# Layer 3's product banks summed by GpSimd adds alone, beside moved spreads and merge

## The chip, the cores and the metric

The kernel runs on one core of one Trainium2 chip. The metric is the device time of one launch in microseconds, the median of several runs. The engines are named as in the profile: PE (TensorE), DVE (VectorE), ACT (ScalarE), POOL (GpSimd), and SP, which only issues transfers.

## The reference

A batch of 512 rows takes 48 embeddings of width 32 each, and passes them through three layers of a compressed interaction network. Each layer makes all products of its input's rows with the 48 original rows, multiplies them with a weight matrix and applies a relu. The sums over the width go through a small dense tower.

```python
def _cin_layer(xi, x0, W, b):
    Wr = W.reshape(Fi, F0, -1)
    out = jnp.einsum('nie,nje,ijo->noe', xi, x0, Wr) + b[None, :, None]
    return jax.nn.relu(out)
x0 = inputs                      # [512, 48, 32]
xs = [x0]
for W, b in ((W1, b1), (W2, b2), (W3, b3)):      # 128 outputs each
    xs.append(_cin_layer(xs[-1], x0, W, b))
return jnp.concatenate(xs, axis=1).sum(axis=-1)
```

## The kernel before

The work is cut into 128 tiles, one for each block of 128 batch rows (4) and each place in the width (32). A tile is a 128 x 48 slice `xx[:, t, :]` of scaled embeddings. Five engines each run the same software pipeline of steps `v` from -4 to 127. In step `v` layer 3 works on tile `v`, layer 2 on tile `v + 1`, layer 1 on tiles `v + 2` and `v + 3`. A step has 24 items, numbered `n`: items 0 to 11 are layer 2, items 12 to 23 are layer 3. In each item PE makes a bank `y` of 128 x 512 (four output groups, one for each of four original rows) in one of five PSUM banks (`RING = 5`), so PE can be at most five items ahead of whoever empties them.

In the code `layer` 0 is layer 2 and `layer` 1 is layer 3. Each bank has to be multiplied by four columns of `xx` and summed into 128 x 128. Two engines share this. `TAKES` says who takes which bank. For a bank of DVE's, four multiply-adds (`fma`) run from PSUM into one of two chains. For a bank of ACT's, `products` writes four scaled pieces into an SBUF buffer `work`, and POOL has to add the banks up. Layer 2 has six banks of ACT's (items 0, 2, 4, 6, 8, 10), layer 3 has five (items 13, 15, 17, 19, 21).

POOL's order in one step, written out by hand in `step` of the gpsimd block, is this:

- `sum_all(1, v - 1)`: finish the previous tile's layer 3 sum, once its DMA has landed (L359, L361, L368, L372)
- `add_by_dma(0, v + 1)`: an accumulating DMA that adds banks 2 and 3 of layer 2 to banks 0 and 1 (L332)
- `x0_scaled` in even steps (L400), and a gather of one embedding field for a later block in odd steps (L300), in steps 1 to 8 in the even ones too
- `sum_rest(0, v + 1)` (L343, L348, L351), and `x0_lo` in even steps (L405)
- `sum_all(0, v + 1)`: wait for the DMA, then L359, L361, L365, L372. The last one writes `psum` of layer 2
- `add_by_dma(1, v)` (L332), `squares_lo` (L394, one for each tile), another gather (L300), one `spread` of 8 tiles where a block has landed (L309, twelve in all), and `sum_rest(1, v)` (L348)

The 144 gathers of blocks 1 to 3 are given out one by one: two in each of steps -3 to 8, and then three in two steps, so that the last one is in step 88. A gather is an indirect DMA issued by POOL. A `spread` turns gathered rows around into tiles of `xx` and scales them; the first block's are made by DVE (L797).

DVE's `merge(layer, t, i)` adds the two chains and `psum`. The one of layer 2 stands at item 20. The one of layer 3's previous tile stands at item 9 (L859 and L864). ACT may write a product bank of the next tile only once `psum` of that layer is done (`s_sum`). PE may write bank `n` only once the bank five items before it is emptied (`bank_free`).

Of the kernel before, what the change touches and what calls it, by code (L numbers as in the profile page):

```python
# [30 lines left out]
F = len(ROWS)  # L31
E = 32
B = 512
P = 128
# [26 lines left out]
FOLDED = (P, 2 * P)  # L61
SUMS = [n + (w == P) for n, w in zip(NA, FOLDED)]
CHUNKS = (1, 0, 2, 3)
PIECES = 4
SPREAD, GROUP, EARLY = 8, 12, 8
# [15 lines left out]
def build(nc, ids, tables, ctx_in, select, pairs_of, w_pair, w_pair_t, w2, w3, b_cin, wt1, bt1, wt2, bt2, wt3, out):  # L81
# [3 lines left out]
    with ExitStack() as stack:  # L85
# [16 lines left out]
        emb = sb("emb", [P, NB, F, E])  # L102
# [19 lines left out]
        mx0, sc0 = sb("mx0", [P, 2, 2]), sb("sc0", [P, 2])  # L122
        mpsq, msq = sb("mpsq", [P, 2]), sb("msq", [P, 2])
# [19 lines left out]
        rest = [sb(f"rest{l}", [P, 2 * P]) for l in (2, 3)]  # L143
# [43 lines left out]
        s_xx = sem("xx_tiles")  # L187
# [7 lines left out]
        s_dma = [sem(f"products{l}_added") for l in (2, 3)]  # L195
        s_last = sem("last_sums")
# [100 lines left out]
        def _(pool):  # L297
            def gather(b, fields, landed=None):
                for f in fields:
                    pool.indirect_dma_start(  # L300
                        emb[:, b, f, :], None, tables[f],
                        bass.IndirectOffsetOnAxis(ap=ids_sb[:, b, f:f + 1], axis=0)).then_inc(landed or s_gather[b], 16)
# [17 lines left out]
            for f, landed in zip(range(0, F, GROUP), s_first):  # L320
                gather(0, range(f, f + GROUP), landed)

# [4 lines left out]
            def add_by_dma(layer, tile):  # L327


                p = prods[layer]  # L330
                written(layer, tile, 2 * ADDED - 1)
                pool.dma_start(p[:, 0:ADDED, :], p[:, ADDED:2 * ADDED, :], accum_op=ALU.add).then_inc(s_dma[layer], 16)  # L332

            def sum_rest(layer, tile):


                s, n = s_sum[layer], tile * SUMS[layer]
                a = prods[layer][:, 2 * ADDED, :]
                wait(pool, s, n)
                written(layer, tile, 2 * ADDED)  # L340
                for m in range(2 * ADDED + 1, NA[layer]):
                    written(layer, tile, m)
                    pool.tensor_tensor(part[layer][:], a, prods[layer][:, m, :], ALU.add).then_inc(s, 1)  # L343
                    a = part[layer][:]
                    n += 1
                    wait(pool, s, n)
                r = rest[layer]
                pool.tensor_tensor(r[:], a[:, 0:2 * P], a[:, 2 * P:4 * P], ALU.add).then_inc(s, 1)  # L348
                if FOLDED[layer] == P:
                    wait(pool, s, n + 1)  # L350
                    pool.tensor_tensor(r[:, 0:P], r[:, 0:P], r[:, P:2 * P], ALU.add).then_inc(s, 1)  # L351

            def sum_all(layer, tile):

                s, n = s_sum[layer], (tile + 1) * SUMS[layer] - 4
                p, a, w = prods[layer], part[layer], FOLDED[layer]
                wait(pool, s_dma[layer], (tile + 1) * 16)
# [5 lines left out]
                r = rest[layer][:, 0:w]  # L363
                if w == P:
                    pool.tensor_tensor(a[:, 0:P], a[:, 0:P], a[:, P:2 * P], ALU.add).then_inc(s, 1)  # L365
                    last = (a[:, 0:P], r)
                else:
                    pool.tensor_tensor(a[:, 0:2 * P], a[:, 0:2 * P], r, ALU.add).then_inc(s, 1)  # L368
                    last = (a[:, 0:P], a[:, P:2 * P])
                wait(pool, s, n + 3)  # L370
                wait(pool, s_m[layer], tile)
                pool.tensor_tensor(psum[layer][:], *last, ALU.add).then_inc(s, 1)  # L372

            def sum_last(layer, tile):


                p, a = prods[layer], part[layer]
                written(layer, tile, 1)
                wait(pool, s_sum[layer], tile * SUMS[layer])
                pool.tensor_tensor(a[:], p[:, 0, :], p[:, 1, :], ALU.add).then_inc(s_last, 1)  # L380
                for m in range(2, NA[layer]):
                    written(layer, tile, m)
                    wait(pool, s_last, m - 1)
                    pool.tensor_tensor(a[:], a[:], p[:, m, :], ALU.add).then_inc(s_last, 1)
                wait(pool, s_last, NA[layer] - 1)
                pool.tensor_tensor(a[:, 0:2 * P], a[:, 0:2 * P], a[:, 2 * P:4 * P], ALU.add).then_inc(s_last, 1)
                wait(pool, s_last, NA[layer])
                wait(pool, s_m[layer], tile)
                pool.tensor_tensor(psum[layer][:], a[:, 0:P], a[:, P:2 * P], ALU.add).then_inc(s_sum[layer], SUMS[layer])

# [18 lines left out]
            columns = [(b, e) for b in range(1, NB) for e in range(0, E, SPREAD)]  # L409
            given_out = {"rows": 0, "columns": 0}  # L410
# [8 lines left out]
            def next_spread(asked):  # L419


                i = given_out["columns"]
                if i < len(columns) and asked >= columns[i][0] * F:
                    spread(*columns[i], SPREAD)
                    given_out["columns"] += 1

            def step(v, parity):

                t0, t2, t3 = v + 3, v + 1, v
                asked = given_out["rows"]  # L430
                if active(t3 - 1):
                    sum_all(1, t3 - 1)
                if active(t2):
                    add_by_dma(0, t2)
                if parity == 0 and active(v + 4):
                    x0_scaled(v + 4)
                if v > 0 and (parity == 1 or v <= EARLY):
                    next_gather()
                if active(t2):
                    sum_rest(0, t2)  # L440
                if parity == 0 and active(v + 4):
                    x0_lo(v + 4)
                if active(t2):
                    sum_all(0, t2)
# [14 lines left out]
            sum_last(1, TILES - 1)  # L459
# [149 lines left out]
        def _(act):  # L609
# [73 lines left out]

            def save_turned(c):

                k = F + CTX if c == 0 else P
                act.wait_ge(s_tt, CHUNKS.index(c) + 1)
                nc.scalar.activation(hT[0:k, c, :], turned[c][0:k, :], ACT.Copy).then_inc(s_tts, 1)

            def step(v, parity):  # L690
# [5 lines left out]
                for n in range(2 * BANKS):  # L696
# [38 lines left out]
        def _(dve):  # L735
# [59 lines left out]
            def spread(g, e0, e1):  # L795
                fields = slice(g * GROUP, (g + 1) * GROUP)
                return nc.vector.tensor_scalar(xx[:, e0:e1, fields], emb[:, 0, fields, e0:e1].rearrange("p f e -> p e f"),  # L797
                                               wpow[:, 0:1], None, ALU.mult)

            for g in range(F // GROUP - 1):  # L800
                dve.wait_ge(s_first[g], 16 * GROUP)
                spread(g, 0, E)
            dve.wait_ge(s_first[F // GROUP - 1], 16 * GROUP)
            for e0, e1 in ((0, 4), (4, E)):
                spread(F // GROUP - 1, e0, e1).then_inc(s_xx, e1 - e0)
# [93 lines left out]
            def x0_over_e(b, i):  # L899
                fields = slice(i * F // PIECES, (i + 1) * F // PIECES)  # L900
                nc.vector.tensor_reduce(low[:, b, fields], emb[:, b, fields, :], axis=AX.X, op=ALU.add).then_inc(s_low, 1)

            def step(v, parity):
                t1, t2, t3 = v + 2, v + 1, v
                other = 1 - parity
                for n in range(2 * BANKS):
# [3 lines left out]
                    for k in range(Q):  # L910
# [20 lines left out]
                        if n == 11 and k == 0 and active(t3 - 1):  # L931
                            over_e(2, t3 - 1)
# [88 lines left out]
```

## Time and profile before

| What | us |
|---|---|
| median of 3 runs | 2412.47 |
| lowest and highest | 2411.84, 2414.49 |
| the profiled execution, its own time | 2416.4 |
| its span in the trace | 2414.6 |
| busy: PE, DVE, ACT, POOL | 2319.0, 2221.3, 2118.3, 1989.4 |

The own time lies 1.8 us over the span. Busy time of an engine counts the time in which an instruction runs. Register, branch and semaphore instructions don't count, and so a busy share below the whole can still leave no room.

### The profile page before, as it was taken

How to read it: one execution, taken by the hardware profiler on the slowest of the kernel's cores; microseconds unless marked ns; L12 is line 12 of the kernel's file. 1: busy time of each engine (PE TensorE's matmuls, PEld its weight loads, DVE VectorE, ACT ScalarE, POOL GpSimd, SP SyncE). 2: the span in 40 equal slices, each digit the busy share in tenths (PEclk: the TensorE clock that was granted, in tenths of full speed). 3: DMA queues.
4: the chain of work that ended last, by engine and by line, in shares of the span. 5: the costliest groups of instructions: out<-in, count | busy, mean ns of one | idle time of the engine just before them, and what ended most of it. 6: DMA issues, size and time to landing. Idle time of an engine off the chain costs nothing.

```text
span 2414.6 us, 67586 instructions
## 1 busy us (share of the span) xinstructions
PE 2319.0 (96%) x14174; PEld 1183.8 (49%) x14174; DVE 2221.3 (92%) x8840; ACT 2118.3 (88%) x7910; POOL 1989.4 (82%) x2262
## 2 busy tenths in 40 slices
PE   1699999999999999999999999999999999999999
PEld 0345555554455555555445555555445555555553
DVE  6499999999999999999999999999999999999995
ACT  4588999998899999899889999899899999999995
POOL 7588888888888888888888888888887777777774
PEclk6799999999999999999999999999999999999999
DMA  5133333333333333333333333333333333333331
GB/s 172 29 72 66 70 71 72 65 69 71 63 71 72 67 68 72 70 69 66 70 63 72 71 72 67 67 72 71 62 71 69 71 65 67 70 70 71 66 68 37
DMA packets 150185, 168.19 MB, mean 70 GB/s; under 512 B 111940, under 2 KB 115655, under 8 KB 150120
## 3 DMA queue, kind: packets, MB, share of 16 engines
q0 software_dynamic: 42864, 136.87, 30.6%
q1 hardware_dynamic: 107256, 30.73, 5.7%
q14 instruction: 57, 0.47, 0.1%
q8 instruction: 8, 0.13, 0.0%
HBM read 12.82 MB, written 0.00 MB: 5 GB/s over the span
## 4 chain that ended last, share of the span: by engine, by line
PE 75%; POOL 8%; issue 7%; ACT 6%; DMA 2%; SPq 1%; DVE 1%; ACTq 0%; DVEq 0%; POOLq 0%
PE y L519 64%; PE m L509 7%; ACT work L633 4%; PE m L491 2%; POOL part L359 2%; DMA work<-work 2%; POOL part L361 1%; POOL emb L300 1%; POOL rest L348 1%; DVE acc L850 1%; POOL work L332 1%; POOL part L343 1%; ACT work L663 1%; POOL psum L372 1%; POOL xx L309 0%
## 5 line engine op out<-in xcount | busy, mean ns | idle before, releaser
L519 PE MATMUL y<-whi,xT 128*128 128x512 f16 x6144 | 2001.2, 380 | 14.9 <-DVE acc L850 9.1
L633 ACT ACTIVATE work<-y,xc 128x128 f32<-128x128 f32 x5632 | 1614.7, 423 | 202.8 <-PE y L519 188.1
L850 DVE SCALAR_TENSOR_TENSOR acc<-y,xc,acc 128x128 f32<-128x128 f32 x5632 | 1628.6, 343 | 54.5 <-PE y L519 47.8
L519 PE MATMUL y<-wlo,xT 128*128 128x512 f16 x3072 | 1165.0, 379 | 0.0
L519 PEld LDWEIGHTS y<-whi,xT 128*128 128x128 f16 x6144 | 599.2, 98 | 658.1 <-issue 55.4
L519 PEld LDWEIGHTS y<-wlo,xT 128*128 128x128 f16 x3072 | 300.9, 98 | 229.1
L359 POOL TENSOR_TENSOR part<-work 128x512 f32<-128x512 f32 x255 | 324.2, 1271 | 68.4 <-DMA work<-work 45.3
L394 POOL TENSOR_TENSOR zl<-work,zh 128x1152 f16<-128x1152 f32 x128 | 344.4, 2691 | 8.1 <-ACT work L663 8.1
L332 POOL DMA_DIRECT2D work<-work x255 | 230.8, 905 | 104.7 <-ACT work L633 104.2
L300 POOL DMA_INDIRECT emb<-tbl,ids_sb x192 | 200.5, 1044 | 46.6 <-issue 45.2
L343 POOL TENSOR_TENSOR part<-work 128x512 f32<-128x512 f32 x128 | 163.6, 1278 | 88.1 <-ACT work L633 85.3
L661 ACT ACTIVATE zh<-m 128x512 f16<-128x512 f32 (+1 forms) x384 | 215.9, 562 | 3.0 <-PE m L491 3.0
L663 ACT ACTIVATE work<-m 128x512 f32<-128x512 f32 (+1 forms) x384 | 218.3, 568 | 0.0
L361 POOL TENSOR_TENSOR part<-part 128x256 f32<-128x256 f32 x255 | 185.6, 728 | 20.0
L491 PE MATMUL m<-x0T,sel 96*128 96x128 f16 x1280 | 136.0, 220 | 53.7 <-DMA x0T<-x0hl 43.7
L491 PEld LDWEIGHTS m<-x0T,sel 96*128 96x128 f16 x1280 | 103.2, 98 | 147.0 <-issue 50.7
L850 DVE SCALAR_TENSOR_TENSOR ends<-y,xc,acc 128x128 f32<-128x128 f32 x512 | 156.0, 351 | 0.0
L509 PE MATMUL m<-w1l,zh 128*128 128x128 f16 x1152 | 127.7, 220 | 0.0
L509 PEld LDWEIGHTS m<-w1l,zh 128*128 128x128 f16 x1152 | 92.0, 99 | 60.3 <-issue 0.8
L509 PEld LDWEIGHTS m<-w1h,zh 128*128 128x128 f16 x1152 | 87.0, 99 | 62.7 <-issue 2.2
L859 DVE TENSOR_TENSOR msum<-ends,psum 128x128 f32<-128x128 f32 x256 | 73.7, 288 | 45.7 <-POOL psum L372 40.6
L509 PE MATMUL m<-w1h,zh 128*128 128x128 f16 x1152 | 107.5, 221 | 1.3 <-ACT work L663 1.3
(108 smaller groups left out, 2141.8 us busy)
## 6 DMA issues: line engine op xcount, KB each, us to landing
work<-work POOLq DMA_DIRECT2D x255, 512.0 KB, 4.8
xT<-hi SPq DMA_TRANSPOSE x256, 2.2
xT<-lo SPq DMA_TRANSPOSE x256, 2.2
emb<-tbl,ids_sb POOLq DMA_INDIRECT x192, 2.5
xx<-w SPq DMA_DIRECT2D x4, 768.0 KB
work<-w SPq DMA_DIRECT2D x4, 768.0 KB
x0T<-x0hl SPq DMA_TRANSPOSE x128, 2.2
wt_sb<-W_top SPq DMA_DIRECT2D x1, 768.0 KB
```

The costliest lines, as they stand in the source:

```text
L300: pool.indirect_dma_start(emb[:, b, f, :], None, tables[f], bass.IndirectOffsetOnAxis(ap=ids_sb[:, b, f:f + 1], axis=0)).then_inc(landed o ...
L332: pool.dma_start(p[:, 0:ADDED, :], p[:, ADDED:2 * ADDED, :], accum_op=ALU.add).then_inc(s_dma[layer], 16)
L359: pool.tensor_tensor(a[:], p[:, 0, :], p[:, 1, :], ALU.add).then_inc(s, 1)
L361: pool.tensor_tensor(a[:, 0:2 * P], a[:, 0:2 * P], a[:, 2 * P:4 * P], ALU.add).then_inc(s, 1)
L394: pool.tensor_tensor(zl[:], zT[:, 0:KF, :], zh[:], ALU.subtract).then_inc(s_zl, 1)
L491: ins = nc.tensor.matmul(misc[PAIR_BANK[g]][:, (k % 4) * P:(k % 4 + 1) * P], sel[:, k * P:(k + 1) * P], x0T[0:2 * F, :], start=True, stop= ...
L509: ins = nc.tensor.matmul(misc[0][:, 0:P], z, w, start=i == 0, stop=i == L1_PASSES - 1)
L519: ins = nc.tensor.matmul(dst[:], xT[layer][:, parity, a, :], w[layer][:, cols], start=i == 0, stop=i == 2)
L633: nc.scalar.activation(prods[layer][:, a, k * P:(k + 1) * P], bank[:, k * P:(k + 1) * P], ACT.Copy, scale=xc[layer][:, parity, j:j + 1]).t ...
L661: nc.scalar.activation(zh[:, 4 * g:4 * g + n, :].rearrange("p t c -> p (t c)"), misc[PAIR_BANK[g]][:, 0:n * P], ACT.Square, scale=SQUARE)
L663: nc.scalar.activation(zT[:, 4 * g:4 * g + n, :].rearrange("p t c -> p (t c)"), misc[PAIR_BANK[g]][:, 0:n * P], ACT.Square, scale=SQUARE). ...
L850: ins = nc.vector.scalar_tensor_tensor(dst, y, col, mine, ALU.mult, ALU.add)
```

## The change

Three things change. The spreads leave POOL and DVE: `emb` is laid out so that all tiles of a field lie side by side, and ACT makes two tiles of `xx` in each odd step, behind its products of item 10, for the tiles `v + 5` and `v + 6`. POOL only raises a semaphore when a block has landed (three short memsets, and one for block 0). DVE makes just the first two tiles. The merge of layer 3 moves on DVE from item 9 to item 11, and `lo_part` by one place. And layer 3's accumulating DMA, `sum_rest` and `sum_all` go: `sum_banks` takes their place at the end of POOL's step. It adds the five banks one after the other into `part`, as ACT writes them, and folds the result twice. It is the order that `sum_last` had for the last tile alone.

```diff
-            def spread(b, e0, n):
-                t0 = b * E + e0
-                src = emb[:, b, :, e0:e0 + n].rearrange("p f e -> p e f")
-                pool.wait_ge(s_gather[b], 16 * F)
-                pool.tensor_scalar(xx[:, t0:t0 + n, :], src, wpow[:, 0:1], None, ALU.mult).then_inc(s_xx, n)
+            def block_landed():
+                pool.memset(flag[:], 0.0).then_inc(s_block, 1)
...
+            def sum_banks(tile):
+                s, n = s_sum[1], tile * SUMS[1]
+                p, a = prods[1], part[1]
+                wait(pool, s, n)
+                written(1, tile, 1)
+                pool.tensor_tensor(a[:], p[:, 0, :], p[:, 1, :], ALU.add).then_inc(s, 1)
+                for m in range(2, NA[1]):
+                    written(1, tile, m)
+                    wait(pool, s, n + m - 1)
+                    pool.tensor_tensor(a[:], a[:], p[:, m, :], ALU.add).then_inc(s, 1)
+                wait(pool, s, n + NA[1] - 1)
+                pool.tensor_tensor(a[:, 0:2 * P], a[:, 0:2 * P], a[:, 2 * P:4 * P], ALU.add).then_inc(s, 1)
+                wait(pool, s, n + NA[1])
+                wait(pool, s_m[1], tile)
+                pool.tensor_tensor(psum[1][:], a[:, 0:P], a[:, P:2 * P], ALU.add).then_inc(s, 1)
...
             def step(v, parity):
...
-                if active(t3 - 1):
-                    sum_all(1, t3 - 1)
                 if active(t2):
-                    add_by_dma(0, t2)
+                    add_by_dma(t2)
...
-                if active(t3) and t3 < TILES - 1:
-                    add_by_dma(1, t3)
                 if active(t0):
                     squares_lo(t0)
                 if v > -4:
                     next_gather()
                 if -4 < v <= 0:
                     next_gather()
-                next_spread(asked)
-                if active(t3) and t3 < TILES - 1:
-                    sum_rest(1, t3)
+                next_block(asked)
+                if active(t3):
+                    sum_banks(t3)
...
+            def spread(t):                       # on ACT
+                wait(act, s_block, (t >> 5) + 1)
+                wait(act, s_xx, t)
+                nc.scalar.activation(xx[:, bass.ds(t, 2), :], emb[:, :, bass.ds(t, 2)].rearrange("p f e -> p e f"),
+                                     ACT.Copy, scale=wpow[:, 0:1]).then_inc(s_xx, 2)
...
+                    if n == 10 and parity == 1 and active(v + 5):
+                        spread(v + 5)
...
-                        if n == 9 and k % 2 == 0 and active(t3 - 1):
-                            merge(1, t3 - 1, k // 2)
                         if n == 9 and active(t1):
-                            if k == 1:
+                            if k == 2:
                                 lo_part(0, t1)
...
-                        if n == 11 and k == 0 and active(t3 - 1):
-                            over_e(2, t3 - 1)
+                        if n == 11 and active(t3 - 1):
+                            if k in (0, 2):
+                                merge(1, t3 - 1, k // 2)
+                            if k == 3:
+                                over_e(2, t3 - 1)
```

The first place is on POOL, from the last instruction of layer 2's sum in one step to layer 2's DMA in the next, in a step of the middle of the program. Here is what stood there before. `part` and `rest` are POOL's partial sums, `psum` its result, `zl` the low part of the squares, and both DMAs on `work` are the accumulating ones.

```order
L372 TENSOR_TENSOR psum<-part,rest 128x128
L332 DMA work<-work 128x1024
L394 TENSOR_TENSOR zl<-work,zh 128x1152
L300 DMA emb<-tbl,ids_sb 128x32
L348 TENSOR_TENSOR rest<-work 128x256
L359 TENSOR_TENSOR part<-work 128x512
L361 TENSOR_TENSOR part<-part 128x256
L368 TENSOR_TENSOR part<-part,rest 128x256
L372 TENSOR_TENSOR psum<-part 128x128
L332 DMA work<-work 128x1024
```

And here is the same place now, with the changed kernel's line numbers.

```order
L364 TENSOR_TENSOR psum<-part,rest 128x128
L387 TENSOR_TENSOR zl<-work,zh 128x1152
L299 DMA emb<-tbl,ids_sb 128x32
L373 TENSOR_TENSOR part<-work 128x512
L377 TENSOR_TENSOR part<-part,work 128x512 x3
L379 TENSOR_TENSOR part<-part 128x256
L382 TENSOR_TENSOR psum<-part 128x128
L332 DMA work<-work 128x1024
```

One DMA, one add over 512 elements and three smaller adds have become four adds over 512 and two smaller ones.

The second place is on DVE, at items 9 and 11. `msum` and the second `ends<-ends,msum` are the two halves of layer 3's merge, `lo` is what layer 2's next input needs, and `acc` and `ends<-y` are the running multiply-adds. Before:

```order
L850 SCALAR_TENSOR_TENSOR acc<-y,xc,acc 128x128 x3
L859 TENSOR_TENSOR msum<-ends,psum 128x128
L850 SCALAR_TENSOR_TENSOR acc<-y,xc,acc 128x128
L890 SCALAR_TENSOR_TENSOR lo<-m,sc,hi 128x128
L850 SCALAR_TENSOR_TENSOR acc<-y,xc,acc 128x128
L864 TENSOR_TENSOR ends<-ends,msum 128x128
L850 SCALAR_TENSOR_TENSOR acc<-y,xc,acc 128x128
L897 SCALAR_TENSOR_TENSOR pooled<-m,pooled 128x128
L850 SCALAR_TENSOR_TENSOR acc<-y,xc,acc 128x128
L897 SCALAR_TENSOR_TENSOR pooled<-ends,pooled 128x128
```

Now:

```order
L844 SCALAR_TENSOR_TENSOR acc<-y,xc,acc 128x128 x5
L884 SCALAR_TENSOR_TENSOR lo<-m,sc,hi 128x128
L844 SCALAR_TENSOR_TENSOR acc<-y,xc,acc 128x128
L891 SCALAR_TENSOR_TENSOR pooled<-m,pooled 128x128
L844 SCALAR_TENSOR_TENSOR acc<-y,xc,acc 128x128
L853 TENSOR_TENSOR msum<-ends,psum 128x128
L844 SCALAR_TENSOR_TENSOR acc<-y,xc,acc 128x128
L844 SCALAR_TENSOR_TENSOR ends<-y,xc,acc 128x128
L858 TENSOR_TENSOR ends<-ends,msum 128x128
L844 SCALAR_TENSOR_TENSOR ends<-y,xc,acc 128x128
L891 SCALAR_TENSOR_TENSOR pooled<-ends,pooled 128x128
```

The merge stands four multiply-adds later than before, with nothing added.

## Rows read from the trace of the kernel before

**Rows 1.** The page: busy time, share and instructions of each engine.

```profile
PE 2319.0 (96%) x14174; PEld 1183.8 (49%) x14174; DVE 2221.3 (92%) x8840; ACT 2118.3 (88%) x7910; POOL 1989.4 (82%) x2262
```

**Rows 2.** Windows, a late stretch: PE, PEld, DVE, ACT, POOL busy; clock, DMA, GB/s.

```profile
1795.00:2344.00 549.00, 548.83 (x3410) 283.11 (x3410) 531.10 (x2140) 502.84 (x1906) 423.58 (x496) 1.00 0.37 69
```

**Rows 3.** Timeline of POOL: L394 of steps 1, 89 and 124 (start, length).

```profile
140.76 2.71 POOL L394 TENSOR_TENSOR zl<-work,zh 128x1152 f16<-128x1152 f32 x1
...
1722.58 2.68 POOL L394 TENSOR_TENSOR zl<-work,zh 128x1152 f16<-128x1152 f32 x1
...
2344.57 2.69 POOL L394 TENSOR_TENSOR zl<-work,zh 128x1152 f16<-128x1152 f32 x1
```

**Rows 4.** Timeline of POOL, one cycle up to an odd step, with a spread.

```profile
1164.82 0.88 POOL L332 DMA_DIRECT2D work<-work  x1 [0.68 <-ACT work L633]
1165.42 2.69 POOL L394 TENSOR_TENSOR zl<-work,zh 128x1152 f16<-128x1152 f32 x1
1168.28 1.08 POOL L300 DMA_INDIRECT emb<-tbl,ids_sb  x1 [0.17 <-issue]
1169.39 1.62 POOL L309 TENSOR_SCALAR xx<-emb,wpow 128x384 f32<-128x384 f32 x1
1170.96 0.74 POOL L348 TENSOR_TENSOR rest<-work 128x256 f32<-128x256 f32 x1
1171.84 1.27 POOL L359 TENSOR_TENSOR part<-work 128x512 f32<-128x512 f32 x1
1173.19 0.73 POOL L361 TENSOR_TENSOR part<-part 128x256 f32<-128x256 f32 x1
1174.00 0.72 POOL L368 TENSOR_TENSOR part<-part,rest 128x256 f32<-128x256 f32 x1
1174.80 0.46 POOL L372 TENSOR_TENSOR psum<-part 128x128 f32<-128x128 f32 x1
1175.20 0.93 POOL L332 DMA_DIRECT2D work<-work  x1
...
1180.31 1.27 POOL L359 TENSOR_TENSOR part<-work 128x512 f32<-128x512 f32 x1
...
1183.40 0.93 POOL L332 DMA_DIRECT2D work<-work  x1
```

**Rows 5.** Timeline of POOL, the even step behind it.

```profile
1193.85 0.92 POOL L332 DMA_DIRECT2D work<-work  x1
...
1195.64 1.27 POOL L343 TENSOR_TENSOR part<-work 128x512 f32<-128x512 f32 x1 [0.49 <-ACT work L633]
...
1198.90 1.27 POOL L359 TENSOR_TENSOR part<-work 128x512 f32<-128x512 f32 x1 [0.32 <-DMA work<-work]
```

**Rows 6.** Timeline of POOL, `sum_last` of the last tile.

```profile
2388.01 1.27 POOL L380 TENSOR_TENSOR part<-work 128x512 f32<-128x512 f32 x1 [3.30 <-ACT work L633]
2389.42 4.11 POOL L384 TENSOR_TENSOR part<-part,work 128x512 f32<-128x512 f32 x3
2393.61 0.72 POOL L386 TENSOR_TENSOR part<-part 128x256 f32<-128x256 f32 x1
2394.47 0.45 POOL L389 TENSOR_TENSOR psum<-part 128x128 f32<-128x128 f32 x1
```

**Rows 7.** Timeline of POOL, an even step of the first eight.

```profile
148.93 0.94 POOL L332 DMA_DIRECT2D work<-work  x1
...
155.05 1.27 POOL L359 TENSOR_TENSOR part<-work 128x512 f32<-128x512 f32 x1 [0.61 <-DMA work<-work]
```

**Rows 8.** Timeline of POOL, layer 3's DMA and its wait, late.

```profile
2078.02 0.88 POOL L332 DMA_DIRECT2D work<-work  x1 [0.89 <-ACT work L633]
...
2082.64 1.27 POOL L359 TENSOR_TENSOR part<-work 128x512 f32<-128x512 f32 x1 [0.66 <-DMA work<-work]
```

**Rows 9.** Groups of instructions, each shape apart: ACT.

```profile
L633 ACT ACTIVATE work<-y,xc 128x128 f32<-128x128 f32 x5632 | 1614.7, 423 | 202.8 <-PE y L519 188.1 <-issue 9.3
...
L639 ACT ACTIVATE x0hl<-xs 128x96 f16<-128x96 f32 x64 | 19.6, 306 | 16.9 <-POOL xs L400 16.9
```

More of the change, by code:

```diff
@@ L59 @@
 ADDED = 2
-FOLDED = (P, 2 * P)
-SUMS = [n + (w == P) for n, w in zip(NA, FOLDED)]
+SUMS = [NA[0] + 1, NA[1] + 1]
 CHUNKS = (1, 0, 2, 3)
 PIECES = 4
-SPREAD, GROUP, EARLY = 8, 12, 8
+GROUP, EARLY = 12, 8
 W1_SETUP = 8
@@ L194, in build @@
         s_zst, s_zl = sem("stacked_squares_ready"), sem("squares_lo")
-        s_dma = [sem(f"products{l}_added") for l in (2, 3)]
-        s_last = sem("last_sums")
+        s_dma = sem("products2_added")
         s_mpsq = sem("x0_unit_squared")
@@ L321, in _ @@
                 gather(0, range(f, f + GROUP), landed)
+            for landed in s_first:
+                pool.wait_ge(landed, 16 * GROUP)
+            block_landed()
             def written(layer, tile, m):
                 wait(pool, s_prod[layer], tile * PRODS[layer] + (m + 1) * Q)
[L327 to L332, printed above, removed]
@@ L334, in sum_rest, with add_by_dma @@
-            def sum_rest(layer, tile):
-                s, n = s_sum[layer], tile * SUMS[layer]
-                a = prods[layer][:, 2 * ADDED, :]
-                wait(pool, s, n)
[L340 to L344, printed above, removed]
+            def add_by_dma(tile):
+                p = prods[0]
+                written(0, tile, 2 * ADDED - 1)
+                pool.dma_start(p[:, 0:ADDED, :], p[:, ADDED:2 * ADDED, :], accum_op=ALU.add).then_inc(s_dma, 16)
@@ L345, in sum_rest @@
+            def sum_rest(tile):
+                s, n = s_sum[0], tile * SUMS[0]
+                a, r = prods[0][:, 2 * ADDED, :], rest[:]
+                wait(pool, s, n)
+                written(0, tile, 2 * ADDED)
+                for m in range(2 * ADDED + 1, NA[0]):
+                    written(0, tile, m)
+                    pool.tensor_tensor(part[0][:], a, prods[0][:, m, :], ALU.add).then_inc(s, 1)
+                    a = part[0][:]
                     n += 1
                     wait(pool, s, n)
-                r = rest[layer]
@@ L348, in sum_rest @@
                 pool.tensor_tensor(r[:], a[:, 0:2 * P], a[:, 2 * P:4 * P], ALU.add).then_inc(s, 1)
[L349 to L357, printed above, removed]
+                wait(pool, s, n + 1)
@@ L358, in sum_all @@
+                pool.tensor_tensor(r[:, 0:P], r[:, 0:P], r[:, P:2 * P], ALU.add).then_inc(s, 1)
+            def sum_all(tile):
+                s, n = s_sum[0], (tile + 1) * SUMS[0] - 4
+                p, a = prods[0], part[0]
+                wait(pool, s_dma, (tile + 1) * 16)
                 wait(pool, s, n)
@@ L362, in sum_all @@
                 wait(pool, s, n + 2)
[L363 to L369, printed above, removed]
-                wait(pool, s, n + 3)
-                wait(pool, s_m[layer], tile)
@@ L372, in sum_all @@
[L372 to L389, printed above, removed]
+                pool.tensor_tensor(a[:, 0:P], a[:, 0:P], a[:, P:2 * P], ALU.add).then_inc(s, 1)
@@ new lines, in sum_all @@
+                wait(pool, s, n + 3)
+                wait(pool, s_m[0], tile)
+                pool.tensor_tensor(psum[0][:], a[:, 0:P], rest[:, 0:P], ALU.add).then_inc(s, 1)
+            def sum_banks(tile):
[13 more added lines that the diff above has]
+                pool.tensor_tensor(psum[1][:], a[:, 0:P], a[:, P:2 * P], ALU.add).then_inc(s, 1)
@@ L408, in _ @@
             rows = [(b, f) for b in range(1, NB) for f in range(F)]
-            columns = [(b, e) for b in range(1, NB) for e in range(0, E, SPREAD)]
-            given_out = {"rows": 0, "columns": 0}
+            given_out = {"rows": 0, "blocks": 1}
             def next_gather():
@@ L417, in next_gather, with next_block @@
                     given_out["rows"] += 1
[L419 to L425, printed above, removed]
+            def next_block(asked):
+                b = given_out["blocks"]
+                if b < NB and asked >= b * F:
+                    pool.wait_ge(s_gather[b], 16 * F)
+                    block_landed()
+                    given_out["blocks"] += 1
             def step(v, parity):
@@ L793, in _ @@
                                         ALU.subtract).then_inc(s_setup, 1)
[L795 removed]
+            for g in range(F // GROUP):
                 fields = slice(g * GROUP, (g + 1) * GROUP)
[L797 to L800 removed]
                 dve.wait_ge(s_first[g], 16 * GROUP)
[L802 to L805, printed above, removed]
+                ins = nc.vector.tensor_scalar(xx[:, 0:2, fields], emb[:, fields, 0:2].rearrange("p f e -> p e f"),
+                                              wpow[:, 0:1], None, ALU.mult)
+            ins.then_inc(s_xx, 2)
             def x0_scale(t, i):
```

16 lines of the change are left out of this document (8 added, 8 removed).

## The prediction

> **What bounds the kernel now.** I read the page's busy shares first, then windows, then POOL's timeline. The shares [rows 1] name PE: 2319.0 of 2414.6 us busy, and DVE, ACT and POOL at 92, 88 and 82%. An average over the span hides who sets the pace where, so the windows come next. In a late stretch without gathers and spreads [rows 2] PE is busy for 548.83 of 549.00 us. It issues 110 matmuls in a step (24 items of three, 10 pair sums, 28 of layer 1), and 3410 of them are 31 steps, so PE alone needs 549.0 / 31 = 17.71 us for a step. Nothing that the change touches can make a step shorter than that. The clock is granted in full there (1.00).
>
> `squares_lo` (L394) runs once in a step, so the distance of two of its starts counts steps. From step 1 to step 89 it is 1722.58 - 140.76 = 1581.8 us, or 17.98 us a step [rows 3]. That is the part in which POOL gathers. From step 89 to step 124 it is 622.0 us for 35 steps, or 17.77. The kernel is thus within 0.27 us a step of PE's floor, and all that the spreads and gathers cost today is 88 x 0.27 = 24 us and 35 x 0.06 = 2 us.
>
> Where POOL has a spread too, POOL sets the pace. The reader should look at the starts in [rows 4]: from 1164.82 to 1183.40 no instruction waits for another engine, the next one always starts within 0.1 us of the end of the one before or behind an "issue" gap of a DMA (0.17 before L300), and the cycle takes 18.58 us, 0.87 more than PE needs. This is the row to price the change from, since busy time leaves out what lies between two dependent adds: L359 lasts 1.27 us, but the add behind it starts 1.35 us after it.
>
> **What the change takes from POOL.** Layer 3's work goes from that cycle [rows 4]: the DMA's issue, 1165.42 - 1164.82 = 0.60 us; L348, 1171.84 - 1170.96 = 0.88; L359 to L372, 1175.20 - 1171.84 = 3.36. Together that is 4.84 us a step. The spread goes too, 1170.96 - 1169.39 = 1.57 us, but only in twelve steps. Without them the odd cycle is 18.58 - 4.84 - 1.57 = 12.17 us.
>
> **What it adds to POOL.** Four adds over 512 elements, a fold and a last add. Their spacings are in [rows 4]: 1.35 (L359 to L361), 0.81 (L361 to L368), 0.40 (L372 to the DMA behind it). The first add stands behind a gather, where I take 1.38. So 1.38 + 3 x 1.35 + 0.81 + 0.40 = 6.64 us. The very same instructions stand at the end of the kernel before [rows 6], and there they are spaced wider: 2389.42 - 2388.01 = 1.41, 4.11 + 0.08 = 4.19 for three, and 0.86 from fold to last add. By these three gaps between adds and the one before the last are 0.06 us longer each, and the part costs 6.64 + 0.24 = 6.88. I can't tell from the trace which holds in a steady step, so I take the middle, 6.76, and keep both ends. POOL's net is 6.76 - 4.84 = +1.92 us a step.
>
> The odd step is then 12.17 + 6.76 = 18.93 us. The even step differs between layer 2's DMA and the L359 that needs it. In the odd step POOL fills this with its own work, 1180.31 - 1175.20 = 5.11 us [rows 4]. In the even one it has less work there and waits for the landing: 1198.90 - 1193.85 = 5.05 [rows 5]. So the even step is 18.93 - 5.11 + 5.05 = 18.87, and the mean is 18.90 us, 1.19 over PE's floor. In steps 1 to 8 the even one has a gather more and its landing is later, 155.05 - 148.93 = 6.12 [rows 7]; I take 5.8 as the mean of those four steps, since own work fills part of them, so 19.6.
>
> Nothing softens this. POOL's queue is in order, and its step ends with `sum_banks`. Behind it waits layer 2's DMA of the next tile, behind that layer 2's sum, and for that sum DVE's merge at item 20. DVE stalls there, PE runs on for five banks and then stalls too. Other loops are shorter than 18.9 us. The longest I find is from `psum` of layer 2 over DVE, PE and ACT's product of item 10 to L343. It took 1195.64 - 1183.40 = 12.2 us in [rows 4, 5], and POOL with its banks is back at L343 after about 10.6 + 1.4 = 12.0 in an even step. The 0.2 us that this leaves is covered by the wait for the landing behind it.
>
> **What lies beside other work.** ACT makes 63 spreads over 96 elements. The nearest row is L639, 96 elements at 306 ns, at the same place of the even steps [rows 9]. The read has a stride of 512 bytes, which no row shows, so it could be up to twice that. ACT idles 188.1 us before its products waiting for PE [rows 9], 1.5 us a step, and so I cost it at nothing; uncovered it would be 63 x 0.3 = 19 us. The merge moved from item 9 to 11 costs nothing if `psum` of layer 3 is there by then: POOL has it some 10.5 us behind layer 2's, and ACT has item 10's product 12.2 us behind it (above), so that DVE should be at item 11 at about 11 us. That is close, and at item 9 it would have waited. DVE's first spreads save about 0.5 us at the start.
>
> **The sum.** Steps 1 to 8: 4 x (18.93 + 19.6) = 154.1. Steps 9 to 88: 80 x 18.90 = 1512.0. Together 1666.1 against 1581.8, so +84.3 us. Steps 89 to 123 have no gathers. An even step loses one, 1.11 us (L300 to L309) and the gap of 0.17 ahead of it [rows 4], and comes to 18.87 - 1.28 = 17.6 us; an odd one loses two and then waits for the landing as the even one does. That is just under PE's 17.71: 35 x 17.71 = 619.9 against 622.0, or -2.1. Start and end: -0.5. The sum is +81.7 us. The profiled execution's own time was 2416.4, which makes 2498; the runs' median is 3.9 us lower than that execution, and the difference carries over: 2412.5 + 81.7 = 2494. I say 2492, a little to the side of the cheaper adds.
>
> **A page's price.** The row says 1.27 us for an add over 512 elements. The Trainium skill (GPSIMD Engine Reference, section 3, Performance versus the Vector engine) gives 4497 ns for one over 2048, and recommends against GpSimd for such adds. A quarter of that is 1.12 us as an estimate from the page. With it the four adds would be 0.6 us cheaper, a step 18.3 us, and the sum about +30 us. The rows of this case have 1.27 us in every such add [rows 4, 6], and they decide.
>
> **The rivals.**
> - The change is a gain: POOL hides the banks, PE stays the bound, and the spreads' cost goes. All 123 steps at 17.71 are 2178 us against 2203.8, so -26 us, 2387. It needs POOL's step at or below 17.71. With 18.9 from above, each of the four adds would have to be spaced 1.08 us or less rather than 1.35 to 1.41. For it speaks that POOL's busy share is only 82% [rows 1], and that the adds come as the products do. Against it is the cycle without a wait in [rows 4]. 8%.
> - POOL's cycle is shorter than I think. The layer 2 DMA lands earlier, since layer 3's no longer shares the queue: 4.62 us is seen for the other DMA late in the kernel [rows 8]. Even steps then take 18.4, and with adds at 1.35 the mean is 18.5, +57 us, 2469. That is my own forecast's lower end. A still shorter cycle, between no change and 2445, I give 2%, and no change within the measurement's 0.2% (4.8 us) 3%.
> - The landing is later. POOL now issues layer 2's DMA beside other transfers, SP's transposes of layer 2's input. At 6.12 [rows 7] in every step, the step is 18.93 + 1.01 = 19.9 us, +165 us, 2578. A landing of 5.5 gives 19.3 us and +118, 2530. It speaks against this that the 6.12 comes with a gather right behind the DMA in an even step, and odd steps with a gather show no wait at 5.11. 6% for over 2535.
> - POOL's late `psum` of layer 3 stalls DVE at item 11 by more than I allow. Some tenths in 80 steps are 20 us more, inside the range.
>
> **How the numbers follow.** POOL as the bound of the gathering steps at 18.5 to 19.3 us and prices between the bounds above has 81%. The bounds give it 2465 to 2535, and a range of 2445 to 2535 leaves out the gain (8%), no change (3%), the little below 2445 (2%) and the late landings (6%), 19% in all. Faster by over 0.2% has 0.08, the same 0.03, slower 0.89; 0.2% is about what a measurement of this kernel tells from no change.
>
> **What would show it.** In the changed kernel's windows, PE's busy share in steps 9 to 88 is about 17.7 / 18.9 = 94%, and about all of the time behind them. POOL has hardly a wait there but the even steps' for the DMA, L394 comes every 18.9 us and then every 17.7, and DVE's `msum` waits for `psum` of layer 2 in most of these steps. The four adds are spaced 1.35 to 1.41. The forecast is wrong if L394 comes every 17.7 to 18 us while gathers still run, or if POOL's timeline shows landings far from 5 us.

## The result and the profile after

The changed kernel takes 2467.45 us (median of 4 runs, 2467.29 to 2467.58), the kernel before 2413.41 in the same comparison. The ratio is 1.0222, with a 95% interval of 1.0209 to 1.0234: slower by 2.2%. The profiled execution took 2467.47 us, its span is 2465.6, against 2414.6 before.

These are the page's busy line and, from its groups, the two of POOL's bank adds, the squares and DVE's merges. Compare the first with [rows 1].

```profile
PE 2325.9 (94%) x14174; PEld 1179.7 (48%) x14174; DVE 2228.2 (90%) x8839; ACT 2147.7 (87%) x7973; POOL 2137.8 (87%) x2254
...
L377 POOL TENSOR_TENSOR part<-part,work 128x512 f32<-128x512 f32 x384 | 487.0, 1268 | 56.9 <-POOL part L377 1.8
L387 POOL TENSOR_TENSOR zl<-work,zh 128x1152 f16<-128x1152 f32 x128 | 303.5, 2371 | 8.2 <-ACT work L651 8.1
...
L853 DVE TENSOR_TENSOR msum<-ends,psum 128x128 f32<-128x128 f32 x256 | 73.6, 287 | 95.0 <-POOL psum L364 90.1
```

POOL's busy share is 87%, which looks like room. The profile page's line by engine of the chain that ended last says otherwise: before, it was PE for 75% and POOL for 8%.

```profile
POOL 48%; PE 27%; issue 10%; DMA 9%; ACT 4%; SPq 1%; DVE 0%; POOLq 0%; ACTq 0%; DVEq 0%
```

The same starts of `squares_lo` as in [rows 3] count the steps. They are those of steps 1, 89 and 124 in POOL's timeline.

```profile
139.37 2.37 POOL L387 TENSOR_TENSOR zl<-work,zh 128x1152 f16<-128x1152 f32 x1
...
1772.53 2.37 POOL L387 TENSOR_TENSOR zl<-work,zh 128x1152 f16<-128x1152 f32 x1
...
2393.97 2.37 POOL L387 TENSOR_TENSOR zl<-work,zh 128x1152 f16<-128x1152 f32 x1
```

Steps 1 to 88 take 1633.2 us (18.56 each) against 1581.8, so +51.4. Steps 89 to 123 take 621.4 against 622.0. The start is 1.4 us shorter (139.37 against 140.76), the end 1.6 longer (from the last start to the span's end 71.6 against 70.0). The sum is the +51.0 us of the spans: the loss lies in the steps that gather, and nowhere else. The windows say the same. Their columns are those of [rows 2]. PE is busy 96.6% in steps 9 to 88 and 99.8% behind them.

```profile
290.34:1772.53 1482.19, 1432.07 (x8801) 723.14 (x8800) 1362.40 (x5480) 1322.18 (x4962) 1338.36 (x1402) 1.00 0.21 39
1789.98:2393.97 603.99, 602.55 (x3741) 310.65 (x3740) 583.91 (x2343) 557.33 (x2108) 511.50 (x544) 1.00 0.21 39
```

This is POOL's timeline from layer 2's last add in one step over an even step, to layer 2's DMA of the next. It answers to [rows 4, 5].

```profile
1216.62 0.45 POOL L364 TENSOR_TENSOR psum<-part,rest 128x128 f32<-128x128 f32 x1
1217.03 2.37 POOL L387 TENSOR_TENSOR zl<-work,zh 128x1152 f16<-128x1152 f32 x1
1219.55 0.97 POOL L299 DMA_INDIRECT emb<-tbl,ids_sb  x1
1220.52 1.29 POOL L373 TENSOR_TENSOR part<-work 128x512 f32<-128x512 f32 x1
1221.95 4.10 POOL L377 TENSOR_TENSOR part<-part,work 128x512 f32<-128x512 f32 x3
1226.13 0.73 POOL L379 TENSOR_TENSOR part<-part 128x256 f32<-128x256 f32 x1
1226.94 0.45 POOL L382 TENSOR_TENSOR psum<-part 128x128 f32<-128x128 f32 x1
1227.34 0.97 POOL L332 DMA_DIRECT2D work<-work  x1
1227.98 0.71 POOL L393 TENSOR_TENSOR xs<-xx,sc 128x96 f32<-128x96 f32 x1
1228.48 1.44 POOL L343 TENSOR_TENSOR part<-work 128x512 f32<-128x512 f32 x1
...
1231.21 0.37 POOL L398 TENSOR_TENSOR x0hl<-xs,x0hl 128x96 f16<-128x96 f32 x1
1232.32 1.27 POOL L357 TENSOR_TENSOR part<-work 128x512 f32<-128x512 f32 x1 [0.74 <-DMA work<-work]
...
1235.41 2.38 POOL L387 TENSOR_TENSOR zl<-work,zh 128x1152 f16<-128x1152 f32 x1
1237.93 1.06 POOL L299 DMA_INDIRECT emb<-tbl,ids_sb  x1
1238.95 1.34 POOL L373 TENSOR_TENSOR part<-work 128x512 f32<-128x512 f32 x1
...
1245.80 0.92 POOL L332 DMA_DIRECT2D work<-work  x1
```

The only wait in this pair of steps is the one for the landing of layer 2's DMA. None stands before L373 or L377: the banks are there before POOL comes to them, so it does not add them "as they come". From DMA to DMA it takes 1245.80 - 1227.34 = 18.46 us.

### The profile page after: what moved, and what is told of

Its sections match the earlier page's. It is cut to its first block, busy times and chain, and to the rows that moved or that the text cites. A ratio compares the mean times of both kernels' runs of the same rounds, so it can differ in the third digit from the quotient of the medians.

```text
span 2465.6 us, 68069 instructions
## 1 busy us (share of the span) xinstructions
PE 2325.9 (94%) x14174; PEld 1179.7 (48%) x14174; DVE 2228.2 (90%) x8839; ACT 2147.7 (87%) x7973; POOL 2137.8 (87%) x2254
## 4 chain that ended last, share of the span: by engine, by line
POOL 48%; PE 27%; issue 10%; DMA 9%; ACT 4%; SPq 1%; DVE 0%; POOLq 0%; ACTq 0%; DVEq 0%
PE y L507 23%; POOL part L377 13%; DMA work<-work 8%; POOL zl L387 8%; POOL part L357 4%; POOL part L373 4%; POOL emb L299 4%; PE m L497 3%; ACT work L621 3%; POOL part L359 3%; POOL part L343 2%; POOL part L379 2%; POOL part L361 2%; POOL work L332 1%; POOL rest L347 1%
## 5 line engine op out<-in xcount | busy, mean ns | idle before, releaser
L844 DVE SCALAR_TENSOR_TENSOR acc<-y,xc,acc 128x128 f32<-128x128 f32 x5632 | 1612.2, 343 | 52.9 <-PE y L507 43.2
L377 POOL TENSOR_TENSOR part<-part,work 128x512 f32<-128x512 f32 x384 | 487.0, 1268 | 56.9 <-POOL part L377 1.8
L387 POOL TENSOR_TENSOR zl<-work,zh 128x1152 f16<-128x1152 f32 x128 | 303.5, 2371 | 8.2 <-ACT work L651 8.1
L299 POOL DMA_INDIRECT emb<-tbl,ids_sb x192 | 194.9, 1015 | 44.4 <-issue 30.2
L343 POOL TENSOR_TENSOR part<-work 128x512 f32<-128x512 f32 x128 | 172.1, 1344 | 60.4 <-ACT work L621 60.3
L357 POOL TENSOR_TENSOR part<-work 128x512 f32<-128x512 f32 x128 | 162.6, 1270 | 46.2 <-DMA work<-work 37.2
L373 POOL TENSOR_TENSOR part<-work 128x512 f32<-128x512 f32 x128 | 165.4, 1292 | 5.0 <-ACT work L621 4.4
L844 DVE SCALAR_TENSOR_TENSOR ends<-y,xc,acc 128x128 f32<-128x128 f32 x512 | 168.4, 352 | 0.0
L853 DVE TENSOR_TENSOR msum<-ends,psum 128x128 f32<-128x128 f32 x256 | 73.6, 287 | 95.0 <-POOL psum L364 90.1
L332 POOL DMA_DIRECT2D work<-work x128 | 118.1, 923 | 12.3 <-ACT work L621 12.3
```

What stands on the lines that cost most here:

```text
L299: pool.indirect_dma_start(emb[:, f, b * E:(b + 1) * E], None, tables[f], bass.IndirectOffsetOnAxis(ap=ids_sb[:, b, f:f + 1], axis=0)).then ...
L343: pool.tensor_tensor(part[0][:], a, prods[0][:, m, :], ALU.add).then_inc(s, 1)
L387: pool.tensor_tensor(zl[:], zT[:, 0:KF, :], zh[:], ALU.subtract).then_inc(s_zl, 1)
L844: ins = nc.vector.scalar_tensor_tensor(dst, y, col, mine, ALU.mult, ALU.add)
```

## The experiments

All are timed beside the kernel before on the same chip, which had medians of 2411.9 to 2413.5 us. "Steps 1 to 88" is read from `squares_lo`, as above. The gathers of the changed kernel and its layer 2 DMA are in all of them except where said.

### The two halves of the change apart

`e1_spreads` keeps the spreads on ACT and the moved merge, and sums layer 3 as before. `e2_banks` is the kernel before with `sum_banks` alone.

```diff
 # e1_spreads, against the changed kernel (POOL)
+                if active(t3 - 1):
+                    sum_all(1, t3 - 1)
...
+                if active(t3) and t3 < TILES - 1:
+                    add_by_dma(1, t3)
...
-                    sum_banks(t3)
+                    sum_rest(1, t3)
```

> The changed kernel with layer 3's accumulating DMA, sum_rest and sum_all put back: the spreads on ACT and the moved merge alone. If GpSimd's own work sets the pace only through the banks, this is bound by TensorE nearly throughout: steps 1 to 88 at about 17.75 us in place of 17.98, 2390 to 2397 us. If the 63 spreads on ACT (about 0.3 us each) lie on the path, it is 2405 to 2415.

> The kernel before with sum_banks for layer 3 alone; spreads stay on GpSimd, the merge at item 9. If GpSimd's occupancy sets the step, the twelve spreads of 1.6 us come on top of the changed kernel's time, eight of them in steps that it bounds and four behind them: 2480 to 2488 us. If the loss comes from the spreads on ACT or the moved merge, this is at about 2413.

| Kernel | us | ratio to before, 95% interval | steps 1 to 88 | squares |
|---|---|---|---|---|
| `e1_spreads` | 2412.58 | 1.0003 (0.9993 to 1.0012) | 1584.5 | 2.69 |
| `e2_banks` | 2484.70 | 1.0303 (1.0286 to 1.0321) | 1647.5 | 2.37 |

The loss is the banks': alone they cost 3.0%. The twelve spreads come on top, as forecast. But the spreads and the merge alone gain nothing. There I had forecast 2390 to 2397, and 2412.58 lies in the range of the other reading, in which the spreads on ACT lie on the path.

### Why the spreads' gain is missing

In `e1_spreads` the twelve slow steps are gone, but a pair of ordinary steps takes 35.9 us rather than 35.55. ACT's timeline in an odd step shows the price of a spread: it holds ACT for 1246.02 - 1245.67 = 0.35 us between the products of item 10 and the squares. ACT has no idle time from there up to item 19, for which layer 3's DMA waits. The products behind the spread are those of item 13, of 15 and 17, and of 19 and 21.

```profile
1244.67 1.16 ACT L635 ACTIVATE work<-y,xc 128x128 f32<-128x128 f32 x4
1245.67 0.51 ACT L691 ACTIVATE xx<-emb,wpow  x1
1246.02 0.65 ACT L663 ACTIVATE zh<-m 128x512 f16<-128x512 f32 x1
...
1246.98 1.21 ACT L635 ACTIVATE work<-y,xc 128x128 f32<-128x128 f32 x4
...
1248.93 2.30 ACT L635 ACTIVATE work<-y,xc 128x128 f32<-128x128 f32 x8
...
1251.60 2.27 ACT L635 ACTIVATE work<-y,xc 128x128 f32<-128x128 f32 x8
```

`e6_spread_item0` moves it, in `e1_spreads`, to a place where ACT idles. `e7_after_item0` moves it in the changed kernel.

```diff
+                    if n == 0 and parity == 1 and active(v + 5):
+                        spread(v + 5)
...
-                    if n == 10 and parity == 1 and active(v + 5):
-                        spread(v + 5)
```

> Spreads and merge alone, with ACT's spread moved from behind the products of item 10 to behind those of item 0, where ACT is idle 0.7 us. If the 0.35 us of the spread delayed the product of item 19, for which layer 3's DMA waits, and this ate the gain of the spreads, the pair of steps is 35.55 again in place of 35.9 and the time 2390 to 2400. If the spreads off GpSimd bring nothing in themselves, it stays at 2412.

> The changed kernel with ACT's spread at item 0. While GpSimd's queue sets the pace ACT's 0.35 us is covered, so this is within 3 us of 2467. If ACT's place had a part in the loss, it is below 2460.

| Kernel | us | ratio to before, 95% interval | steps 1 to 88 |
|---|---|---|---|
| `e6_spread_item0` | 2401.01 | 0.9951 (0.9937 to 0.9964) | 1569.5 |
| `e7_after_item0` | 2468.40 | 1.0224 (1.0208 to 1.0239) | 1634.5 |

With the spread at item 0 the gain is there: 12 us or 0.5%, and this kernel beats both. Its steps 1 to 88 are 15.0 us shorter than those of `e1_spreads`, though the time is 1 us over the range that I gave. In the changed kernel the same move does nothing, since POOL's queue covers it. So the place of the spread is what cost `e1_spreads` its gain. By which path is less sure: DVE's instruction `mx`, of which more below, also takes less time with the spread at item 0 (337 ns in the mean, not 514), and no run separates the two.

### Is it what POOL has to do, or when

`e3_nogather_b` takes work from POOL without touching the banks: it leaves out the gathers of blocks 1 to 3, and all spreads read block 0's first two tiles, so that its result is not the reference's. `e4_merge9` touches only where DVE waits for layer 3.

```diff
 # e3_nogather_b, against the changed kernel
-            rows = [(b, f) for b in range(1, NB) for f in range(F)]
+            rows = []
...
-                if b < NB and asked >= b * F:
-                    pool.wait_ge(s_gather[b], 16 * F)
+                if b < NB and t_now[0] >= 32 * b - 8:
```

```diff
 # e4_merge9, against the changed kernel (DVE)
+                        if n == 9 and k % 2 == 0 and active(t3 - 1):
+                            merge(1, t3 - 1, k // 2)
```

> The changed kernel without the 144 gathers of blocks 1 to 3: the spreads read block 0's first two tiles for all tiles, and the sums over the width read block 0, so the output is not the reference's. If the sum of what GpSimd must do in a step sets the pace, each step falls to TensorE's 17.7 us (the changed kernel has 18.56 in steps 1 to 88) and the time is 2388 to 2398. If the lateness of the last adds sets it, whatever else GpSimd does, it stays over 2440.

> The changed kernel with layer 3's merge and lo_part back at their places of item 9. GpSimd has layer 3's psum about 10.4 us behind layer 2's, and DVE is at item 9 at about 9.7, so DVE should wait there some tenths in each gathering step. If GpSimd's queue alone sets the pace, DVE has room for it: 2465 to 2471 us. If the merge's place matters, the waits come on top: 2480 to 2510.

| Kernel | us | ratio to before, 95% interval | steps 1 to 88 |
|---|---|---|---|
| `e3_nogather_b` | 2389.54 | 0.9900 (0.9885 to 0.9915) | 1558.8 (17.71 each) |
| `e4_merge9` | 2466.74 | 1.0231 (1.0214 to 1.0248) | 1632.8 |

Without gathers the same banks, added at the same place, cost nothing. PE never idles in this window of `e3_nogather_b`:

```profile
290.00:1700.00 1410.00, 1410.00 (x8763) 728.56 (x8762) 1363.45 (x5453) 1304.75 (x4938) 1201.77 (x1278) 1.00 0.21 39
```

So the loss needs both, the banks and the gathers: it is the sum of POOL's work in a step. Taking out the gathers also lets the last add come earlier, so this run alone doesn't exclude that its lateness costs the time. `e4_merge9` speaks against that: with the merge at item 9, DVE waits 54.6 us in steps 9 to 88 for layer 3's `psum` (L382), and the time is the same. `e8_after_extra` below settles it, since its add stands behind layer 3's `psum`.

### The term that was mis-sized

`e5_squares_first` is `e1_spreads` with two lines of POOL's step exchanged.

```diff
-                if active(t3) and t3 < TILES - 1:
-                    add_by_dma(1, t3)
                 if active(t0):
                     squares_lo(t0)
+                if active(t3) and t3 < TILES - 1:
+                    add_by_dma(1, t3)
```

> Spreads and merge alone (layer 3 summed with its DMA), and squares_lo put ahead of that DMA's issue. It tells where the 0.33 us went by which the squares became shorter in the changed kernel. If the instruction behind an accumulating DMA's issue pays for the rest of that issue, the squares take 2.37 us here though the DMA is still there; if the DMA's traffic slows them, they stay at 2.7. The DMA now lands later and layer 3's sum waits for it: about 2.4 + 4.65 + 3.4 us from layer 2's psum to the next DMA and 8.1 on to the next psum, 18.5 us a step and 2470 to 2495 us.

It took 2497.63 us, ratio 1.0349 (1.0333 to 1.0365), 3 us over the forecast's end, and each of steps 1 to 88 took 18.6 us. POOL's timeline:

```profile
1199.50 2.37 POOL L396 TENSOR_TENSOR zl<-work,zh 128x1152 f16<-128x1152 f32 x1
1201.82 0.85 POOL L334 DMA_DIRECT2D work<-work  x1
1202.98 1.07 POOL L301 DMA_INDIRECT emb<-tbl,ids_sb  x1 [0.30 <-issue]
...
1206.76 1.28 POOL L361 TENSOR_TENSOR part<-work 128x512 f32<-128x512 f32 x1 [1.95 <-DMA work<-work]
```

The squares take 2.37 us in all 128 instances. So they are longer by 0.32 us only directly behind the DMA's issue. This run does not yet tell the issue from the DMA's traffic, as I had expected it to, since here both come behind the squares. Two things do. An add made while such a DMA is in flight takes as long as one without: 1.27 us for 512 elements and 0.46 for 128, in the medians of the kernel before. In the changed kernel, L393 directly behind layer 2's DMA takes 0.71 us, and L398, of the same size and still ahead of the landing, 0.37. And the DMA's issue and the squares cost the same in either order: 1202.98 - 1199.50 = 3.48 us from the squares' start to the gather here, and 1168.28 - 1164.82 = 3.46 from the DMA's start to the gather in [rows 4]. So the 0.32 us was the rest of an issue that runs on into the next instruction.

### One add more

An add over 512 elements of constants, into a tile that nobody reads, goes to the end of POOL's step: into the changed kernel and into `e6_spread_item0`.

```diff
+            def one_more_add(t):
+                wait(pool, s_setup, SETUP)
+                wait(pool, s_spare, t)
+                pool.tensor_tensor(spare[:], w1b[:, 0:4, :], w1b[:, 4:8, :], ALU.add).then_inc(s_spare, 1)
```

> The changed kernel with one more add over 512 elements on GpSimd at the end of each step, of constants into a spare tile. If GpSimd's queue has no slack in steps 1 to 88, each of them grows by the whole spacing of such an add, 1.35 to 1.42 us: +119 to +125. Behind them GpSimd's own cycle is 17.2 us by the changed kernel's rows and gets to 18.6, +30. Together 2611 to 2627 us. A time under 2580 would mean that something else shared in setting the pace.

> The same added instruction in the kernel with layer 3's DMA and ACT's spread at item 0 (2401.0 us). Its GpSimd needs about 17.0 us a step for itself where it gathers, 0.8 less than the step, and so only 1.4 - 0.8 = 0.6 us of each add should show in steps 1 to 88 and nothing behind them: 2440 to 2465 us. If GpSimd had no slack there either, it is at 2520 or more; if it had plenty, at 2401.

| Kernel | us | ratio to before, 95% interval | steps 1 to 88 | steps 89 to 123 |
|---|---|---|---|---|
| `e8_after_extra` | 2588.81 | 1.0729 (1.0711 to 1.0747) | 1737.6 | 644.8 |
| `e9_item0_extra` | 2478.25 | 1.0271 (1.0254 to 1.0288) | 1616.7 | 650.0 |

In the changed kernel each of the 88 steps grows by 1.19 us in the profiled execution. That one was 9 us longer than the median, so the growth in the others is nearer to 1.1. It is nearly the whole of what the add takes in the queue there: what stands behind it, which does not use its result, starts 1.21 us after it (median). Layer 3's `psum` is written before this add, so the lateness of the last add has no part in it. The time is 22 us under my range. I had taken 1.35 at least, the spacing of adds that hang on each other, or 119 us, and 30 us for the steps behind 88; the trace has 104 and 23. In the kernel with layer 3's DMA a step grows by only 0.54 us: there POOL had 1.21 - 0.54 = some 0.7 us of slack, as forecast. But its steps behind 88 grew by 0.9 us, where I had forecast nothing.

### What the late steps were waiting for

DVE's timeline of `e9_item0_extra` in a late even step, and POOL's at the same time:

```profile
2168.28 0.34 DVE L862 TENSOR_SCALAR acc<-y,xc 128x128 f32<-128x128 f32 x1
2168.54 2.92 DVE L834 TENSOR_SCALAR mx<-mx 128x2 f32<-128x2 f32 x1
2171.37 0.34 DVE L866 SCALAR_TENSOR_TENSOR acc<-y,xc,acc 128x128 f32<-128x128 f32 x1
```

```profile
2167.96 1.03 POOL L351 TENSOR_TENSOR rest<-work 128x256 f32<-128x256 f32 x1
2168.64 1.56 POOL L397 TENSOR_TENSOR spare<-w1b 128x512 f32<-128x512 f32 x1
2169.87 1.55 POOL L362 TENSOR_TENSOR part<-work 128x512 f32<-128x512 f32 x1
2171.50 0.72 POOL L364 TENSOR_TENSOR part<-part 128x256 f32<-128x256 f32 x1
```

A DVE instruction on two elements in a partition (`x0_scale`, i = 1) takes 2.92 us. The trace shows no semaphore that it waits for. It starts while POOL's L351 runs, and ends at 2171.46, when POOL's second add over 512 elements does (2171.42). Of the 64 such instructions in this run 62 take over 0.25 us, and each of these ends within 0.12 us of the end of one of POOL's. The three last kernels cut it into two instructions of one element each, in `e6_spread_item0`, in `e9_item0_extra` and in the changed kernel.

```diff
-                    nc.vector.tensor_scalar(mx0[:, :, 1], mx0[:, :, 0], TINY0, HALF_RANGE, ALU.max, ALU.mult).then_inc(s, 1)
+                    for c in range(2):
+                        ins = nc.vector.tensor_scalar(mx0[:, c, 1:2], mx0[:, c, 0:1], TINY0, HALF_RANGE, ALU.max, ALU.mult)
+                    ins.then_inc(s, 1)
```

> The kernel with layer 3's DMA and ACT's spread at item 0 (2401.0 us), with DVE's tensor_scalar of two elements (mx) cut into two of one element each. The one of two elements took 337 ns in the mean there, 154 at least and 2009 at most, as long as GpSimd's adds around it. If only the form of two elements waits for GpSimd's adds to end, each of the two takes 145 to 170 ns always. The mean wait that goes is 0.2 us in every other step, much of it covered: 2392 to 2402 us. If one element waits too, their maximum stays near 2 us.

> The same cut in the kernel with GpSimd's additional add beside layer 3's DMA (2478.3 us). There the two-element instruction took 2.92 us in each even step behind step 88, over two adds of GpSimd that stand back to back, and these steps took 19.38 us. If that wait made the late part 31 us longer than without the add, it goes: 2442 to 2452 us. If the late part is bound by GpSimd's occupancy, it stays at 2472 or more.

> The same cut in the changed kernel, where the two-element instruction took 588 ns in the mean. DVE has room while GpSimd's queue sets the pace, so the cut does nothing: 2464 to 2469 us. If DVE's waits for GpSimd's adds had a part in the loss, it is below 2460.

| Kernel | us | ratio to before, 95% interval | `mx`, mean ns before the cut, after it |
|---|---|---|---|
| `e10_item0_split` | 2399.55 | 0.9947 (0.9934 to 0.9961) | 337, 146 |
| `e11_extra_split` | 2451.94 | 1.0161 (1.0145 to 1.0176) | 1021, 145 |
| `e12_after_split` | 2467.76 | 1.0221 (1.0205 to 1.0237) | 588, 146 |

All three times came out in their ranges. In `e11_extra_split` the steps behind 88 take 620.0 us in place of 650.0, 17.7 each, so the unforecast 31 us was this wait. Its steps 1 to 88 are as long as before the cut (1618.7 against 1616.7): those are POOL's. The changed kernel has the wait too, but DVE has room for it. `e10_item0_split` is the fastest of the kernels that do the whole work, though not told apart from `e6_spread_item0`.

## Why the prediction was right, and where it was off

The prediction was 2492 us with a range of 2445 to 2535, slower with a chance of 0.89. The measured 2467.45 lies in it, 25 us under the forecast.

**PE's floor.** 17.71 us a step, from [rows 2]. `e3_nogather_b` runs at 17.71 for 88 steps, and the changed kernel's late steps at 17.76. Right.

**POOL as the bound of the gathering steps.** Right, and shown from both sides: without the gathers the loss is gone, and one add more costs nearly its whole time in each step. The squares come every 18.5 us in steps 9 to 88 and every 17.8 behind them, and DVE's `msum` waits 90.1 us in all for layer 2's `psum`. PE's share in the gathering steps is 96.6% where I had 94. The shorter step alone makes it 17.71 / 18.53 = 95.6%; the rest is that PE's own busy time in a step reads 17.90 us there.

**The length of POOL's step.** This is where the difference comes from. I had 18.87 us for the even step, and it is 18.46. By terms, what I took and what it is:

- From the squares' start to the gather: 1168.28 - 1165.42 = 2.86 [rows 4], and 1237.93 - 1235.41 = 2.52. I took the DMA's issue to cost 0.60 us, the distance from its start to the next one's. It is 0.88 to 0.93, and the rest stood inside the squares behind it. This is the term that was mis-sized: -0.34 us in each step.
- The gather: 1.11, and 1238.95 - 1237.93 = 1.02.
- The banks: 6.76 between bounds of 6.64 and 6.88, and 1245.80 - 1238.95 = 6.85. From the first add to the second it is 1.48 us, wider than I had in either bound. The three adds take 4.17, as in [rows 6], and the fold 0.80, as in [rows 4].
- The landing: 5.05, and 1232.32 - 1227.34 = 4.98. Layer 2's sum is 3.09 in both.

Together -0.41 us in the even step. The mean of steps 9 to 88 is 18.53 us for my 18.90, or 30 us less in 80 steps, and steps 1 to 8 took 151.0 in place of 154.1. The steps behind them took 1.5 us more than I had, and start and end 0.7. So the span grew by 51.0 us, not by 81.7.

That is 31 us too much, and the forecast was off by 25 only because two other things took 6 us back. I had gone 2 us to the side of the cheaper adds. And I had carried over the 3.9 us by which the profiled execution of the kernel before lay above the median; that of the changed kernel lies at its median. The second was luck.

With the landing at 5 us, the rival of a later landing fell. So did that of an early landing, although the measured time is nearly the 2469 us that it gave: its landing of 4.62 us is not there, and the shorter step has the cause above. By its own terms it comes to +54 us rather than +57, since it leaves out the late steps and the start. The two sums of the later landing leave out that steps behind 88 would have grown too.

**ACT's spreads at nothing.** The step of the working was "cost it at nothing", since ACT idles 1.5 us a step. For the changed kernel the sum holds: `e7_after_item0` shows no difference. The reason that I gave doesn't. In the timeline of `e1_spreads` ACT idles ahead of the products of items 2, 4 and 6 (0.68, 0.29 and 0.20 us) and not behind item 10. Where POOL has room the 0.35 us shows on the path (`e1_spreads` against `e6_spread_item0`). The instruction took 0.51 us, not 0.3.

**The merge at item 11.** I said that it would have waited at item 9. It does, 54.6 us in steps 9 to 88 of `e4_merge9`, 0.7 us in each. But the time does not grow by it, so the later place is not needed for this order.

**The price from the Trainium skill** (GPSIMD Engine Reference, section 3, Performance versus the Vector engine), an estimate of 1.12 us for an add, is not what this case has: 1.268 us in the mean of 384.

The net of the banks in POOL's queue is then 6.85 - (0.93 + 0.88 + 3.36) = +1.68 us a step. An ordinary gathering step grew from 17.78 us (half of 35.55) to 18.53, by 0.75, so that POOL had room for some 0.9 us of it. The extra add in `e6_spread_item0` gave some 0.7. The two don't measure quite the same, and the exact slack of the kernel before is left open: the extra add was not put into it.

## What to carry to other kernels

Price a change to an in-order queue from a stretch in which that queue never waits, from start to start, and compare it with the floor of the engine that is the bound: a busy share of 82% hid that 1.7 us more did not fit into a step of 17.8. The issue of a DMA on such a queue costs its whole duration, even if the next instruction seems to start inside it. And work moved to another engine belongs where that engine idles in the step, not where the code has a similar instruction: the same 0.35 us took the gain of the spreads at item 10 and left it at item 0.

## What the runs showed of the hardware

A DVE `tensor_scalar` from SBUF to SBUF with two elements in a partition was seen to wait for POOL's instructions to end, over two adds in a row: 2.92 us with 1.56 and 1.55 us adds beside it, whose records overlap by 0.33 us, against 152 to 160 ns at least. With one element in each of two instructions, none of 128 took over 154 ns in any of three kernels. The wait shows on no semaphore, and in the profile only as an instruction much longer than its fellows: the mean and the median of one form differ (460 ns and 165 ns for L818 in the kernel before). The Trainium skill (SBUF — State Buffer, section SBUF: two separate sides) describes an exclusive lock of a port pair that GpSimd shares with DVE's instructions in a two-port mode, held for a whole instruction. The trace agrees with such a lock, with the 2.92 us, but for one thing: DVE did not get its turn between two adds. In which mode the instruction ran, no trace shows.

The tail of an accumulating DMA's issue runs into the next instruction: 0.32 us of the squares' 2.69, and 0.34 of L393's 0.71. Where the next one is a gather, its record starts only behind the tail, after 0.30 us of "issue" (`e5_squares_first`).
